# Delta rule on one NeuronCore: the narrow products in four column groups, with a copy and a transpose behind each

## What is computed

```python
def gated_delta_rule(q, k, v, g, beta):          # per batch and head
    def step(S, inp):                            # S is 128 x 32
        qt, kt, vt, gt, bt = inp
        S = S * jnp.exp(gt)
        delta = (vt - kt @ S) * bt
        S = S + kt[:, None] * delta[None, :]
        return (S, qt @ S)
```

## Time and profile before

| | |
|---|---|
| median of 3 runs | 1396.35 us (1395.06 to 1400.76) |
| profiled execution | 1392.02 us, its span 1390.2 us |
| PE busy | 1264.7 us, 91% |
| DVE busy | 812.9 us, 58% |
| ACT busy | 548.3 us, 39% |
| POOL busy | 523.1 us, 38% |
| mean granted clock of PE | 0.943 of full speed |

### The profile page before, as it was taken

The page is one execution under the profiler, slowest core; times in us unless marked ns, Lnnn a source line. Parts: engine busy times, 40 slices in busy tenths (PEclk is TensorE's granted clock), DMA queues, the critical chain, the costliest instruction groups (busy, mean ns, idle before and its releaser), DMA issues. The chain is left out here.

```text
span 1390.2 us, 25042 instructions
## 1 busy us (share of the span) xinstructions
PE 1264.7 (91%) x9172; PEld 833.0 (60%) x9172; DVE 812.9 (58%) x1828; ACT 548.3 (39%) x1273; POOL 523.1 (38%) x595
## 2 busy tenths in 40 slices
PE   8999999957977787999999887899999989999998
PEld 4968778735545444677777675455555554344487
DVE  5464655566435665767766424577777774733253
ACT  4554647233122676666676231144433441000010
POOL 3453626531661467567567202322222201600010
PEclk9999999959897898999999867899999999999999
DMA  3010029446866202122121210100001106642100
GB/s 132 25 38 9 29 72 317 173 158 242 228 183 204 68 16 42 22 41 39 26 42 22 34 29 1 65 18 22 21 26 52 39 1 179 190 128 74 30 8 23
DMA packets 144167, 106.57 MB, mean 77 GB/s; under 512 B 87872, under 2 KB 130088, under 8 KB 142912
## 3 DMA queue, kind: packets, MB, share of 16 engines
q1 hardware_dynamic: 135904, 88.31, 22.1%
q0 software_dynamic: 4496, 13.33, 3.4%
q10 hardware_dynamic: 3664, 3.55, 0.8%
HBM read 84.16 MB, written 22.35 MB: 77 GB/s over the span
## 5 line engine op out<-in xcount | busy, mean ns | idle before, releaser
L2845 PE MATMUL la_banks<-la_xe,la_f_w 128*128 128x512 f32 x348 | 153.1, 598 | 3.4 <-DVE la_xe L3223 3.4
L2203 DVE SCALAR_TENSOR_TENSOR dh_front<-dh_pj,df_conv,dh_front 128x510 f32<-128x510 f32 x144 | 107.3, 745 | 76.2 <-ACT dh_front L1942 72.4
L3386 POOL TENSOR_TENSOR la_area<-la_area 128x512 f32<-128x512 f32 x48 | 60.3, 1279 | 173.3 <-DVE la_area L3066 152.9
L2845 PEld LDWEIGHTS la_banks<-la_xe,la_f_w 128*128 128x128 f32 x348 | 66.0, 192 | 84.7 <-issue 84.6
L353 POOL TENSOR_TENSOR wa_qkT<-lf_area 128x512 f32<-128x512 f32 x40 | 50.8, 1271 | 97.6 <-DVE lf_area L325 97.6
L3223 DVE TENSOR_TENSOR la_xe<-xT,la_area 128x1024 f32<-128x1024 f32 x29 | 52.5, 1827 | 56.2 <-PE la_banks L2845 49.8
L2963 ACT ACTIVATE la_area<-la_banks,la_nmax 128x256 f32<-128x256 f32 x128 | 59.0, 475 | 58.6 <-DVE la_nmax L3075 58.6
L357 POOL TENSOR_TENSOR mw_gu<-mw_gu,const 128x384 f32<-128x384 f32 x64 | 63.7, 1001 | 29.9 <-ACT mw_gu L388 29.9
L3406 POOL TENSOR_TENSOR la_o_rstd<-la_o_var,la_minus_half 128x1 f32<-128x1 f32 x8 | 6.4, 805 | 166.0 <-DVE la_o_var L3285 166.0
L2971 ACT COPY la_area<-la_banks 128x512 f32<-128x512 f32 x64 | 37.5, 590 | 56.2 <-PE la_banks L2694 55.9
L280 PE MATMUL wa_po<-wa_wo,mw_rows 128*128 128x256 f32 x256 | 56.6, 379 | 0.0
(11 more groups left out here) (621 smaller groups left out, 3070.2 us busy)
## 6 DMA issues: line engine op xcount, KB each, us to landing
mw_gu<-in_L_ffn_gate_up SPq DMA_DIRECT2D x16, 768.0 KB, 12.6
placed<-mw_rows SPq DMA_DIRECT2D x8, 768.0 KB, 10.8
mw_d<-in_L_ffn_down SPq DMA_DIRECT2D x16, 384.0 KB, 13.2
mw_rows<-placed SPq DMA_DIRECT2D x8, 768.0 KB, 6.5
la_area<-w_table POOLq DMA_DIRECT2D x6, 1024.0 KB, 11.4
pairs<-me_picked SPq DMA_DIRECT2D x7, 704.0 KB, 3.8
la_f_w<-in_L_ffn_q_proj SPq DMA_DIRECT2D x32, 128.0 KB, 2.2
la_f_w<-in_L_ffn_k_proj SPq DMA_DIRECT2D x32, 128.0 KB, 2.5
```

Of the source, the lines that this page charges most:

```text
L2203: dve.scalar_tensor_tensor(dst, src[:, :, 0:SEQ - j], conv[:, a, m, D_CONV - 1 - j:D_CONV - j], dst, ALU.mult, ALU.add).then_inc(tapped, 1)
L2845: mm = pe.matmul(acc[c][m], f_w[n % SLOTS][:, m, k, :], xe[(n - U) % RING][:, k, :], start=first and k == 0, stop=last and k == KC - 1)
L3386: pool.tensor_tensor(qrot[:, c, n, :], prod[:, c, 2 * n, :], prod[:, c, 2 * n + 1, :], ALU.add).then_inc(rotated, 1)
```

## The change

The five products of a head (solution of chunk 0, state, within of chunk 0, solution and within of chunk 1) swap their operands: the 32 columns of values are stationary and the 128x128 matrix moves. The four sequences b write to the four groups of 32 partitions of one 128x128 piece of PSUM (`flat_out`). ACT copies the piece to SBUF (`keep`), into a new buffer `fl`, or for the last head into part of `E`. PE transposes it back (`turn_solution`, `turn_state`, `turn_within`) to where the product stood before, and DVE and ACT read it there as before. The semaphores `flat_done` and `flat_kept` count over the products in order. On DVE `taps(a, 0)` now stands ahead of `first_delta`.

```diff
-        own = sb("own", [P, 2048 - 2 * P])
+        own, fl = sb("own", [P, 2048 - 2 * P]), sb("fl", [P, 3 * P])
+        SOL0, STATE, WITHIN0, SOL1, WITHIN1 = range(5)
+        FLAT_IN, KEPT_AT = (1, 0, 1, 1, 0), (0, 1, 2, 0, 2)
+        flat_out = lambda h, n: bank(h)[:, FLAT_IN[n], P:2 * P]
+        kept = lambda h, n: cut(LAST, P * KEPT_AT[n], P, "p (o n) -> p (o n)", o=1) if h == LAST else fl[:, P * KEPT_AT[n]:P * KEPT_AT[n] + P]
+        nth = lambda h, n: 5 * h + n + 1 if h < LAST - 1 else 5 * (LAST - 1) + 2 * n + (h - LAST + 1) + 1
...
 solution:
-                        mm = pe.matmul(small(h, 1)[:, b, :], TTs(h)[:, BATCH * c + b, :], rhs, start=True, stop=True)
-                    mm.then_inc(sol_done, 1)
+                        mm = pe.matmul(flat_out(h, (SOL0, SOL1)[c])[D_V * b:D_V * b + D_V, :], rhs, TTs(h)[:, BATCH * c + b, :], start=True, stop=True)
+                    mm.then_inc(flat_done, 1)
+
+                def turn_solution(h, c):
+                    pe.wait_ge(flat_kept, nth(h, (SOL0, SOL1)[c]))
+                    pe.transpose(bank(h)[:, 1, 0:P], kept(h, (SOL0, SOL1)[c]), env.c("ident")).then_inc(sol_done, 1)
 state:
-                        mm = pe.matmul(small(h, 0)[:, b, :], k0[h % RINGS["k0"]][:, b, :], DE(h)[:, b, :], start=True, stop=True)
-                    mm.then_inc(s_done, 1)
+                        mm = pe.matmul(flat_out(h, STATE)[D_V * b:D_V * b + D_V, :], DE(h)[:, b, :], k0[h % RINGS["k0"]][:, b, :], start=True, stop=True)
+                    mm.then_inc(flat_done, 1)
 within:
-                        mm = pe.matmul(small(h, 1 - c)[:, b, :], PT[h % RINGS["PT"]][:, BATCH * c + b, :], DL(h)[:, c, b, :], start=True, stop=True)
-                    mm.then_inc(o_done, 1)
+                        mm = pe.matmul(flat_out(h, (WITHIN0, WITHIN1)[c])[D_V * b:D_V * b + D_V, :], DL(h)[:, c, b, :], PT[h % RINGS["PT"]][:, BATCH * c + b, :], start=True, stop=True)
+                    mm.then_inc(flat_done, 1)
...
 ACT:
+                def keep(h, n):
+                    act.wait_ge(flat_done, nth(h, n))
+                    act.copy(kept(h, n), flat_out(h, n)).then_inc(flat_kept, 1)
```

More of the change, by code:

```diff
@@ L1442, in delta_attention @@
             sem(n) for n in ("stats_done", "aggr_done", "var_done", "half_done", "rstd_done", "tile_ready", "x_turned", "x_copied"))
+        flat_done, flat_kept = sem("flat_done"), sem("flat_kept")
         half_gated, half_scaled, recleared = sem("half_gated"), sem("half_scaled"), sem("recleared")
@@ L1775, in state, with turn_state @@
                     for b in range(BATCH):
-                        mm = pe.matmul(small(h, 0)[:, b, :], k0[h % RINGS["k0"]][:, b, :], DE(h)[:, b, :], start=True, stop=True)
-                    mm.then_inc(s_done, 1)
+                        mm = pe.matmul(flat_out(h, STATE)[D_V * b:D_V * b + D_V, :], DE(h)[:, b, :], k0[h % RINGS["k0"]][:, b, :], start=True, stop=True)
+                    mm.then_inc(flat_done, 1)
+                def turn_state(h):
+                    pe.wait_ge(flat_kept, nth(h, STATE))
+                    pe.transpose(bank(h)[:, 0, 0:P], kept(h, STATE), env.c("ident")).then_inc(s_done, 1)
                 def within(h, c):
@@ L1785, in within, with turn_within @@
                     for b in range(BATCH):
-                        mm = pe.matmul(small(h, 1 - c)[:, b, :], PT[h % RINGS["PT"]][:, BATCH * c + b, :], DL(h)[:, c, b, :], start=True, stop=True)
-                    mm.then_inc(o_done, 1)
+                        mm = pe.matmul(flat_out(h, (WITHIN0, WITHIN1)[c])[D_V * b:D_V * b + D_V, :], DL(h)[:, c, b, :], PT[h % RINGS["PT"]][:, BATCH * c + b, :], start=True, stop=True)
+                    mm.then_inc(flat_done, 1)
+                def turn_within(h, c):
+                    pe.wait_ge(flat_kept, nth(h, (WITHIN0, WITHIN1)[c]))
+                    pe.transpose(bank(h)[:, 1 - c, 0:P], kept(h, (WITHIN0, WITHIN1)[c]), env.c("ident")).then_inc(o_done, 1)
                 def carried(h):
@@ L1819, in _ @@
                         turn(b, 3)
+                    for h in chain_heads(i):
+                        turn_solution(h, 0)
                     if a is not None:
@@ L1836, in _ @@
                         k_products(b, 1)
+                    for h in chain_heads(i):
+                        turn_state(h)
                     for l in level_heads(i):
@@ L1848, in _ @@
                         turn_carried(h)
+                    for h in chain_heads(i):
+                        turn_within(h, 0)
                     if a is not None:
@@ L1864, in _ @@
                         k_products(b, 2)
+                    for h in chain_heads(i):
+                        turn_solution(h, 1)
+                    if b is not None:
                         k_products(b, 3)
@@ L1878, in _ @@
                         segment(a, 1)
+                    for h in chain_heads(i):
+                        turn_within(h, 1)
+                    if a is not None:
                         project(a, 3)
@@ L2039, in _ @@
                         silu(b, 3)
+                    for h in chain_heads(i):
+                        keep(h, SOL0)
                     for l in level_heads(i):
@@ L2055, in _ @@
                     for h in chain_heads(i):
+                        keep(h, STATE)
+                    for h in chain_heads(i):
                         copy_state(h)
@@ L2064, in _ @@
                         copy_x5(l)
+                    for h in chain_heads(i):
+                        keep(h, WITHIN0)
                     for h in chain_heads(i):
@@ L2080, in _ @@
                         copy_out(q)
+                    for h in chain_heads(i):
+                        keep(h, SOL1)
                     for l in level_heads(i):
@@ L2090, in _ @@
                         copy_y6(l)
+                    for h in chain_heads(i):
+                        keep(h, WITHIN1)
                     if i == -1:
@@ L2305, in _ @@
                         scales_k(b)
+                    if a is not None:
+                        taps(a, 0)
                     for h in chain_heads(i):
                         first_delta(h)
-                    if a is not None:
-                        taps(a, 0)
                     if i == -1:
```

## The result

| | before | after |
|---|---|---|
| median | 1396.35 us (7 runs, 1394.83 to 1403.06) | 1385.76 us (7 runs, 1382.04 to 1390.95) |
| ratio to before | | 0.992 (95%: 0.990 to 0.994) |
| profiled execution, its span | 1392.02, 1390.2 us | 1384.60, 1382.8 us |
| PE busy | 1264.7 us | 1237.3 us |
| ACT busy | 548.3 us | 557.9 us |

The changed kernel is faster by 10.6 us. The predicted 1383 was 2.8 us low, inside its range.

The account below looks back on a forecast made before the run. PE was taken to bound part A, PE and an ACT and DVE chain part B. Eight rounds at 1.15 us give 9.2, rounds 12 to 14 0, 1.2 and 2.5: 12.9 off 1396.35, so 1383, range 1375 to 1392.

Parts of the forecast that it names:

- What bounds the kernel: Full rounds of the delta stage: PE alone sets part A; PE and an ACT and DVE chain together set part B.
- Part A: Round from turn(b, 2) to within(h, 1), 16.60 us, PE never idle; saving of 1.05 us a round, all on the path.
- part B: Round from within(h, 1) to turn(b, 2), 8.75 us; of 0.76 us PE time saved, only 0.1 shortens the round.
- the wait for silu: PE ahead of turn(b, 2): new idle time of 0.6 to 0.8 us a round, released by silu.
- The price of a product: Each product on PE: 0.36 us instead of 0.91, plus 0.10 a mode switch; within 0 about 0.30, transposes 0.14 each.
- Rival 2: Narrow products on PE cost 0.57 us (passes partly serialise) or switches 0.28; 0.4 us a round, 1391 in all; chance 0.14.
- Which new waits are covered: Copies and transposes after the five products: about 0.6 us each, covered by other work, with slack of 0.3 to 0.4 at the tightest.
- rival 3: Copies not covered, 0.6 us open at each of part A's four turns; 1406 us; chance 0.08 in full or half.
- rival 4: Less active array lowers the clock in full rounds; at 0.93 a round costs 1.8 us more, 1393 to 1398; chance 0.06.
- no idle over 0.2 us before the five turns: Sign on PE in full rounds: no wait above 0.2 us before the transposes of the five products.
- The sum of a round: Full round of the delta stage: 1.05 us from part A plus 0.1 from part B, 1.15 us shorter.
- Rounds 11 to 14: End of the delta stage: savings of 1.15 us in round 11, 0 in 12, 1.2 in 13, 2.5 in 14.

Follow-up runs that it names:

- b_only: Changed kernel with only solution 0 and within 1 in the new form, the other three products old: 1391.77 us, ratio 1.001 to the kernel before.
- mask_split: Changed kernel with POOL's mask_g(a, 0) ahead of the block solve and mask_g(a, 1) right behind it, even rounds: 1385.29 us, ratio 0.991 to before.
- combined: Changed kernel with mask_split, a later copy and transpose of within 1, later second_out, and add_t4 ahead of sums(b, 2): 1386.31 us, ratio 0.990 to before.
- a_only: Changed kernel with solution 0 and within 1 back in the old form, the other three products new: 1388.45 us, ratio 0.996 to the kernel before.
- project_first: Changed kernel with project(a, 3) ahead of both segments on PE and tap0(a, 3) ahead of the exponentials on ACT: 1390.80 us, ratio 0.994 to before.

## Why the prediction was right, by its steps

**What bounds the kernel: right.** Part A gave most of its share and part B little or nothing, and the wait for silu came where and as long as said: 4.5 us in seven rounds, 0.64 each, said 0.6 to 0.8. b_only shows that PE's saving in B comes back as this wait, and ACT's rows show that its work fills B.

**The price of a product: right.** 0.36 us as taken. PE's own saving was 2.04 us a round against 1.81, since the transposes cost 0.11 and not 0.14 and within 0 took 0.24 and not 0.30. Rival 2, with 0.57 a product, fell. An estimate by the Trainium skill, "TensorE: Matmul & The Clock Gate", section "Measured speedup vs the span model", was 0.29 us a product; the trace's 0.36 holds the exit too, and the 0.24 of the product without an exit lies below it.

**Which new waits are covered: right for the five turns, incomplete for the rest.** No turn in a full round waits for its copy more than 0.2 us, so rival 3 fell, and the clock stayed at 1.00, so rival 4 fell. But "no idle over 0.2 us before the five turns" looked only at the new steps. A faster PE reached two old ones that had stood just ready: `segment` behind POOL's mask (0.59 us, even rounds) and `level5_x` behind `add_t4` on DVE (0.60 us, odd rounds). mask_split takes the first away and combined the second, and each time the wait before that step goes.

**The sum of a round: 1.15 said, 0.96 measured.** The terms that were off: A saved 1.19 us (16.51 to 15.32) and not 1.05 in even rounds, but only 0.6 in odd ones (the wait for `add_t4`). B saved 0.26 and not 0.1 where no mask was late, and gave back 0.27 where it was (9.02 against 8.75). Rounds 4 and 5, where the pattern of waits sets in, gained 1.09 and 1.27 us, the later ones 0.8 and 1.0 by turns. Over seven rounds that is 6.7 us where the prediction has 8.05.

**Rounds 11 to 14: 4.9 us said (1.15, 0, 1.2 and 2.5), 3.0 to 6.9 measured** by the two profiles of each kernel (127.9 and 129.6 before, 124.9 and 122.7 after; means 5.0 apart). The split inside was off, both ways. From the `segment` of round 10 to `level4_x` of round 13 nothing was gained: 52.95 us before (747.01 to 799.96), 52.73 after (742.78 to 795.51), 51.7 and 52.7 in the second profiles. Round 11 was counted as one of the full rounds, but like rounds 12 to 14 it has no projections of a head: the last starts at 748.81, in round 10. DVE does have the last head's blocks ready 0.9 us earlier there, 22.0 us behind that segment (764.81) against 23.0 (769.96). But SP, which works in order, has the reads of earlier heads' solved blocks ahead of their store and issues it 24.6 us behind the segment (767.37), where it was 24.4 (771.44). So the gain is gone before the transfer begins.

From round 13 on it was 2.8 to 7.9 us where 3.7 was said, 5.4 by the means of two profiles each and 6.6 by those of all fourteen. State, within 0 and solution 1 give it (a_only against b_only). A product of round 14 costs 0.43 us at the low clock, not 0.6. How the rest divides over the single steps stays open: no run took round 14 apart.

**In all:** 6.7 + 5.0 = 11.7 us by the traces and 10.6 by the medians, against 12.9. That the sum came this close is in part luck: 1.3 us too much in the full rounds and 1.15 in round 11 stand against 1.7 too little from round 13 on.

## What to carry to other kernels

Where a float32 product has few columns to stream, it pays for its passes and not for the columns: a pass over a 128x128 stationary operand takes 0.11 us here with 32 columns streamed, and 0.11 with the 128 of a transpose. With the narrow operand stationary in column groups eight passes cost 0.36 us instead of 0.91, and the copy and transpose back are cheap as long as other work stands between. Before counting an engine's saving, list every step of it that today finds its input just ready, old ones too: two of them took 2.9 of PE's 14.3 us here. And when a round is set by two chains, measure each alone: rearranging one (project_first) can make it longer, where the amount of work on it binds and not its order.

## What the hardware did that I had not expected

The wait for `add_t4` in odd rounds begins one operation earlier. The operation ahead of it on DVE, 128x8 elements, takes 0.17 us in one round and 0.68 in the next. DVE, two rounds:

```profile
633.83 0.17 DVE L2270 TENSOR_SCALAR dh_sse<-dh_ss 128x8 f32<-128x8 f32 x1
...
658.46 0.68 DVE L2270 TENSOR_SCALAR dh_sse<-dh_ss 128x8 f32<-128x8 f32 x1
659.05 1.09 DVE L2292 SCALAR_TENSOR_TENSOR dh_U<-dh_lv,const,dh_U 32x128 f32<-32x128 f32 x3
```

POOL beside the second:

```profile
657.07 2.04 POOL L2466 TENSOR_TENSOR dh_E<-const,dh_par 128x512 f32<-128x512 f32 x2
```

It ends at 659.14, 0.03 us after POOL's pair of 128x512 products (659.11). All seven of the twelve that take over 0.2 us in the changed kernel (0.33 to 1.08) end 0.02 to 0.03 us behind the end of such a product of POOL. The five beside POOL's short products (128x28 and 128x39) of the block solve take 0.17. In combined, where ten of the twelve stand clear of the long products, the median is 0.17:

```profile
L2274 DVE TENSOR_SCALAR dh_sse<-dh_ss x12: 171/171/506, 492.0 to 759.7; 128x8 f32<-128x8 f32 x12
```

In the changed kernel the median is 0.42 us. The Trainium skill, "SBUF — State Buffer", section "Who interferes with whom", says that VectorE and GpSimd share a pair of ports as an exclusive lock, that a `tensor_scalar` in a fast mode asks for it, and that the second to come waits until the first ends. The trace agrees, by the moment at which the operation ends; no run here took POOL's products away to show it. It makes `add_t4` 0.5 us late, most of PE's 0.60. In the kernel before the same operation took between 0.17 and 1.09 us too, and PE came late enough not to wait.
